# Graph attention over 4096 nodes: another half key group transposed by DMA, adjacency loads issued as a pair, masks made later

## The reference

```python
q = x @ Wq.T + bq; k = x @ Wk.T + bk; v = x @ Wv.T + bv      # x: 4096 x 128, float32
scores = q @ k.T / sqrt(128)
scores = where(adj > 0, scores, -9e15)                       # adj: 4096 x 4096, int32
att = softmax(scores, axis=-1) @ v
return layernorm(x + elu(att), eps=1e-5)                     # no scale or shift
```

## Time and profile before

| | |
|---|---|
| median of 3 runs | 438.9 us (438.66 to 438.95) |
| profiled execution | 439.14 us, of which the span from first to last instruction is 437.3 us |
| busy share of the span | PE 97%, DVE 82%, ACT 82%, POOL 79% |
| DMA | 105.29 MB, mean 241 GB/s; 64 DMA transposes, 64 adjacency loads of 1 MB |
| granted TensorE clock | 0.997 |

### The profile page before, as it was taken

How to read it: one execution, slowest core, us unless ns; L and a number is a source line. 1 busy time by engine, 2 the same in 40 slices (tenths; PEclk the granted TensorE clock), 3 DMA queues, 4 the chain that set the end, 5 groups by cost and what they waited for, 6 DMA issues and landing times.

```text
span 437.3 us, 11386 instructions
## 1 busy us (share of the span) xinstructions
PE 423.0 (97%) x3471; PEld 308.8 (71%) x3471; DVE 359.4 (82%) x665; ACT 357.8 (82%) x739; POOL 346.2 (79%) x617
## 2 busy tenths in 40 slices
PE   8998999999999999999999999999999999999974
PEld 5563676677777777777777777777777777777764
DVE  1759988888889888888889898888889998888723
ACT  5778687888888988888888898888888898888992
POOL 0064567898888988898888988889888888889884
PEclk9999999999999999999999999999999999999998
DMA  8822999999999999999999999999999999997553
GB/s 225 374 98 97 202 252 271 264 262 279 289 274 265 261 244 273 263 269 256 253 276 269 264 245 261 279 259 265 244 271 272 266 252 250 275 265 184 96 103 67
DMA packets 152013, 105.29 MB, mean 241 GB/s; under 512 B 135104, under 2 KB 143808, under 8 KB 143808
## 3 DMA queue, kind: packets, MB, share of 16 engines
q1 hardware_dynamic: 151568, 104.94, 91.0%
q10 hardware_dynamic: 432, 0.20, 0.2%
HBM read 69.47 MB, written 2.10 MB: 164 GB/s over the span
## 4 chain that ended last, share of the span: by engine, by line
PE 82%; DMA 5%; SPq 3%; DVE 3%; ACT 2%; issue 2%; POOL 2%; POOLq 0%; ACTq 0%; DVEq 0%
PE ps_out L721 22%; PE ps_scores L682 11%; PE ps_scores L683 11%; PE ps_scores L684 11%; PE ps_out L723 11%; PE ps_t L698 11%; DMA p_turned<-p_rows 4%; SPq L234 3%; PE ps_t L626 2%; DVE scores L528 2%; PE ps_out L637 1%; DMA x_rows<-in_x_dram 1%; PE ps_out L626 1%; PE ps_scores L648 1%; DVE adj L514 1%
## 5 line engine op out<-in xcount | busy, mean ns | idle before, releaser
L290 POOL TENSOR_TENSOR p_rows<-scores,p_rows 128x256 f16<-128x256 f32 x256 | 178.5, 729 | 13.0 <-ACT p_rows L431 13.0
L528 DVE CUSTOM_DVE_ANT_0 scores<-ps_scores,adj 128x1024 f32<-128x1024 f32 x128 | 155.9, 1218 | 14.2 <-issue 10.8
L414 ACT ACTIVATE scores<-scores,neg_max 128x1024 f32<-128x1024 f32 x128 | 145.6, 1138 | 0.0
L543 DVE TENSOR_TENSOR p_lo<-ps_t,p_hi 128x512 f16<-128x512 f32 x128 | 85.0, 684 | 36.7 <-ACT p_hi L423 36.4
L514 DVE TENSOR_SCALAR adj<-adj 128x1024 f32<-128x1024 int32 x128 | 104.8, 818 | 0.8 <-DMA adj<-in_adj_dram 0.7
L721 PE MATMUL ps_out<-v_parts,p_hi 128*128 128x256 f16 x512 | 98.5, 273 | 1.5 <-DVE p_lo L543 1.1
L721 PE MATMUL ps_out<-v_parts,p_turned 128*128 128x256 f16 x512 | 98.0, 273 | 0.6 <-DMA p_turned<-p_rows 0.4
L682 PE MATMUL ps_scores<-k_hi,q_hi 128*128 128x512 f16 x256 | 97.0, 379 | 1.0 <-DVE max_parts L528 0.9
L683 PE MATMUL ps_scores<-k_lo,q_hi 128*128 128x512 f16 x256 | 97.0, 379 | 0.0
L684 PE MATMUL ps_scores<-k_hi,q_lo 128*128 128x512 f16 x256 | 97.0, 379 | 0.0
L723 PE MATMUL ps_out<-v_parts,p_lo 128*128 128x128 f16 x512 | 91.4, 219 | 0.0
(11 more groups left out here) (70 smaller groups left out, 440.4 us busy)
## 6 DMA issues: line engine op xcount, KB each, us to landing
adj<-in_adj_dram SPq DMA_DIRECT2D x64, 1024.0 KB, 5.3
out_dram<-y_out SPq DMA_DIRECT2D x32, 64.0 KB, 4.9
x_rows<-in_x_dram SPq DMA_DIRECT2D x4, 256.0 KB, 4.3
x_rows<-in_x_dram SPq DMA_DIRECT2D x2, 512.0 KB, 6.3
p_turned<-p_rows SPq DMA_TRANSPOSE x64, 4.5
w_rows<-in_L_gnn_Wk_dram ACTq DMA_DIRECT2D x1, 64.0 KB, 2.7
w_rows<-in_L_gnn_Wq_dram ACTq DMA_DIRECT2D x1, 64.0 KB, 3.3
w_rows<-in_L_gnn_Wv_dram ACTq DMA_DIRECT2D x1, 64.0 KB, 4.0
```

The costliest lines, as they stand in the source:

```text
L290: last = nc.gpsimd.tensor_tensor(p_rows[c][:, w:][:, cols], s_sb[s][:, c * PIECE:c * PIECE + w][:, cols], p_rows[c][:, 0:w][:, cols], ALU. ...
L414: nc.scalar.activation(s_sb[s][:, cols], s_sb[s][:, cols], ACT.Exp, bias=neg_max[:, s:s + 1], accum_out=p_sums[:, s, c:c + 1]).then_inc(ex ...
L528: nc.vector.tensor_tensor_reduce(out=s_sb[s][:, cols], in0=ps_scores[c % 2][:, :], in1=mask_sb[s][:, cols], scale=SCALE, scalar=-3.0e38, o ...
L543: nc.vector.tensor_tensor(p_lo[:, k, :], ps_t[bank_of(s, g)][:, :], p_hi[:, k, :], ALU.subtract).then_inc(plo_ready, 1)
```

## The change

Half of group 4 (256 columns) moves from PE's transposes to the DMA transpose of piece 1, which grows from 1024 to 1280 columns; the half group that is left is transposed by PE in two blocks. POOL's low parts stay operations of 256 columns, so `low_rows(1)` has five. Both loads of an adjacency tile are issued one after the other, behind `turn(p-2, n, 1)`. Each mask is made one step ahead of its use, where it was made half a round ahead. PE's transposes and value products get new steps.

```diff
-DMA_COLS = (PIECE, PIECE)
+MIXED_COLS = 256
+DMA_COLS = (PIECE, PIECE + MIXED_COLS)
...
-T_AT = {4: 6, 5: 7, 6: 8, 7: 10}
-PV_ORDER = (4, 5, 6, 0, 1, 7, 2, 3)
+T_AT = {4: 6, 5: 6, 6: 8, 7: 9}
+PV_STEPS = ((5,), (), (6,), (7, 0), (1,), (2,), (3,), (4,))
+PV_ORDER = tuple(g for step in PV_STEPS for g in step)
...
-LOW_PARTS = 4
+LOW_COLS = 256
...
+        def by_pe(g):
+
+            return slice(MIXED_COLS, BANK) if g == MIXED else slice(0, BANK)
...
                 if turns_1:
                     turn(p - 2, n, 1)
-                if head:
+                if loads:
+                    load_half(p + 1, 1 - n, 0, False)
                     load_half(p + 1, 1 - n, 1, False)
                 if stores:
                     store(p - 4, n)
                 if turns_0:
                     turn(p - 1, 1 - n, 0)
-                if loads:
-                    load_half(p + 2, n, 0, False)
...
-                for b in range(LOW_PARTS):
-                    cols = slice(b * w // LOW_PARTS, (b + 1) * w // LOW_PARTS)
+                for b in range(w // LOW_COLS):
+                    cols = slice(b * LOW_COLS, (b + 1) * LOW_COLS)
...
-                    if c < BY_DMA:
-                        dve.wait_ge(rows_lo, BY_DMA * (i - 2) + c + 1)
+                    if 2 * c <= MIXED:
+                        dve.wait_ge(rows_lo, BY_DMA * (i - 2) + min(c + 1, BY_DMA))
...
-                    if j == 1 and has_scores:
-                        mask_piece(p, n, 3)
-                    if j in (3, 5, 7) and has_scores and makes_mask:
-                        mask_piece(p + 1, 1 - n, j // 2 - 1)
+                    if j in (1, 3, 5) and has_scores:
+                        mask_piece(p, n, j // 2 + 1)
+                    if j == 7 and has_scores and makes_mask:
+                        mask_piece(p + 1, 1 - n, 0)
```

More of the change, by code:

```diff
@@ L20 @@
 LOG_P_SCALE = 15.0 * math.log(2.0)
-DMA_COLS = (PIECE, PIECE)
+MIXED_COLS = 256
+DMA_COLS = (PIECE, PIECE + MIXED_COLS)
 BY_DMA = len(DMA_COLS)
 FIRST_PE = sum(DMA_COLS) // BANK
+MIXED = FIRST_PE
 PE_GROUPS = STEPS - FIRST_PE
-T_AT = {4: 6, 5: 7, 6: 8, 7: 10}
-PV_ORDER = (4, 5, 6, 0, 1, 7, 2, 3)
+T_AT = {4: 6, 5: 6, 6: 8, 7: 9}
+PV_STEPS = ((5,), (), (6,), (7, 0), (1,), (2,), (3,), (4,))
+PV_ORDER = tuple(g for step in PV_STEPS for g in step)
 POOL_OPS = 11
-LOW_PARTS = 4
+LOW_COLS = 256
 LAST_OPS = 9
@@ L234, in turn, with period @@
                 sp.dma_start_transpose(p_turned[c][s][:, :, :], p_rows[c][:, :]).then_inc(turned[c], 16)
-            def period(p, n, head=True, turns_0=True, turns_1=True, stores=True, loads=True):
+            def period(p, n, turns_0=True, turns_1=True, stores=True, loads=True):
                 if turns_1:
                     turn(p - 2, n, 1)
-                if head:
+                if loads:
+                    load_half(p + 1, 1 - n, 0, False)
                     load_half(p + 1, 1 - n, 1, False)
@@ L245, in period @@
                     turn(p - 1, 1 - n, 0)
-                if loads:
-                    load_half(p + 2, n, 0, False)
             load(0, 0)
             load(1, 1)
-            period(0, 0, head=False, turns_0=False, turns_1=False, stores=False)
             period(1, 1, turns_1=False, stores=False)
@@ L257, in _ @@
                     period(2 * pair + n, n)
[L258 to L261, removed]
+            period(TILES - 2, 0)
+            period(TILES - 1, 1, loads=False)
+            period(TILES, 0, loads=False)
+            period(TILES + 1, 1, turns_0=False, loads=False)
             store(TILES - 2, 0)
@@ L422, in high_part @@
                     act.wait_ge(pv_done, pv_count(i - 1, g))
-                nc.scalar.activation(p_hi[:, k, :], ps_t[bank_of(s, g)][:, :], ACT.Copy).then_inc(phi_ready, 1)
+                nc.scalar.activation(p_hi[:, k, by_pe(g)], ps_t[bank_of(s, g)][:, by_pe(g)], ACT.Copy).then_inc(phi_ready, 1)
             def high_rows(i, s, c, first):
                 w = DMA_COLS[c]
-                act.wait_ge(exp_done, exp_count(i, c))
+                act.wait_ge(exp_done, exp_count(i, (c * PIECE + w - 1) // PIECE))
                 if not first:
@@ L542, in low_part @@
                 dve.wait_ge(phi_ready, PE_GROUPS * i + k + 1)
-                nc.vector.tensor_tensor(p_lo[:, k, :], ps_t[bank_of(s, g)][:, :], p_hi[:, k, :],
+                nc.vector.tensor_tensor(p_lo[:, k, by_pe(g)], ps_t[bank_of(s, g)][:, by_pe(g)], p_hi[:, k, by_pe(g)],
                                         ALU.subtract).then_inc(plo_ready, 1)
@@ L598, in period @@
                         reciprocal(p - 2, n)
-                    if j == 1 and has_scores:
-                        mask_piece(p, n, 3)
-                    if j in (3, 5, 7) and has_scores and makes_mask:
-                        mask_piece(p + 1, 1 - n, j // 2 - 1)
+                    if j in (1, 3, 5) and has_scores:
+                        mask_piece(p, n, j // 2 + 1)
+                    if j == 7 and has_scores and makes_mask:
+                        mask_piece(p + 1, 1 - n, 0)
             for n in range(AHEAD):
                 low_of_projection(n)
-                if n > AHEAD - PIECES:
-                    mask_piece(0, 0, n - AHEAD + PIECES - 1)
+                if n == AHEAD - 1:
+                    mask_piece(0, 0, 0)
             period(0, 0, has_1=False, has_2=False, warm=False)
@@ L695, in transposes @@
                     pe.wait_ge(plo_ready, PE_GROUPS * i + k - 1)
-                for b in range(BLOCKS):
+                for b in range(by_pe(g).start // P, BLOCKS):
                     kb = g * BLOCKS + b
@@ L704, in values @@
                     pe.wait_ge(plo_ready, PE_GROUPS * i + g - FIRST_PE + 1)
-                elif g % 2 == 0 or pv_count(0, g - 1) > pv_count(0, g):
-                    pe.wait_ge(turned[g // 2], 16 * i + 16)
+                if g <= MIXED and (g % 2 == 0 or pv_count(0, g - 1) > pv_count(0, g)):
+                    pe.wait_ge(turned[min(g // 2, BY_DMA - 1)], 16 * i + 16)
                 if g == PV_ORDER[0] and not first:
@@ L714, in values @@
                     k = g * BLOCKS + b
-                    if g >= FIRST_PE:
+                    c = min(g // 2, BY_DMA - 1)
+                    if b * P >= by_pe(g).start and g >= FIRST_PE:
                         high = p_hi[:, g - FIRST_PE, b * P:(b + 1) * P]
@@ L718, in values @@
                     else:
-                        high = p_turned[g // 2][s][:, g % 2 * BLOCKS + b, :]
-                        low = p_turned[g // 2][s][:, DMA_COLS[g // 2] // P + g % 2 * BLOCKS + b, :]
+                        high = p_turned[c][s][:, k - c * PIECE // P, :]
+                        low = p_turned[c][s][:, DMA_COLS[c] // P + k - c * PIECE // P, :]
                     nc.tensor.matmul(ps_out[s][:, 0:2 * D], high, v_parts[:, k, :],
@@ L741, in period @@
                             transposes(p - 1, 1 - n, g, not warm)
-                    if has_2:
-                        values(p - 2, n, PV_ORDER[j], first)
+                    for g in PV_STEPS[j]:
+                        if has_2:
+                            values(p - 2, n, g, first)
             period(0, 0, has_1=False, has_2=False, warm=False)
```

## The result

The median went from 438.92 us (438.66 to 438.99) to **515.0 us** (514.5 to 515.28), a ratio of 1.173 [1.172, 1.175]. The forecast was 448.8 us, at most 458: the sign was right, the size wrong by a factor of more than seven (+76 for +10).

The account below looks back on a forecast made before the run. PE bounded the kernel, POOL 3.5% behind; the change would make POOL's 12.61 us loop the pace. 439.14 + 8.9 (rounds) + 2.0 (end) - 1.0 (start) = 449.0 us profiled, 448.8 median; range 438 to 458.

Parts of the forecast that it names:

- The step that failed: On PE: two fewer transposes a tile remove 7.0 us in all, leaving 12.0 us a round, with other work unchanged.
- what costs nothing: DVE's smaller low part, masks, load deadlines, new waits of `masked_piece(2)` and `high_rows(1)`, and the later store: no added time.
- the second loop: From the end of `y` through ACT's copies, DVE's low part and masked piece, exponentials and POOL back to `y`: 12.57 us.
- POOL's loop: POOL's own work and waits in a round: 11.80 us before, 11.80 + 0.63 + 0.18 = 12.61 us after the change.
- the two terms that were forecast: On POOL, each round: 0.63 us for one more 256-column operation, and 0.18 us later start behind ACT's longer copy.
- single-operation bound: Lower bound of POOL's round with the added operation and nothing for ACT's longer copy: 12.43 us.
- POOL at some 95%: Sign expected in the middle stretch: POOL busy some 95% of the time.
- the likeliest case: Rounds set by loops of 12.4 to 12.8 us, 443 to 455 us in all; chance 0.56.
- `res` to the end of `y`: Last term in the sum of the second loop, on POOL: 1.80 us.
- (a): Rival: PE sets the round at 12.0 us, 432 us, or 434 with some waiting; chance 0.12.
- (b): Rival: DVE's masks move off POOL's operations into its waits; rounds of 12.2 us, some 437 to 440 us; chance 0.12.
- (c): Rival: the DMA queue becomes the bound at 12.9 to 13.35 us a round; 458, up to 471 us; chance 0.16.

Follow-up runs that it names:

- e9_copy_ahead_of_row_sum: Changed kernel with two places for group 4, group 7's products one step later, and ACT copying piece 1 ahead of `row_sum`: 446.03 us, ratio 1.015.
- e10_mean_on_act: As e9_copy_ahead_of_row_sum, and ACT's row sum gives the negative mean, so POOL's `neg_mean` is left out: 437.15 us, ratio 0.997.
- e5: Changed kernel with two places for group 4 and group 7's value products at step 4 instead of step 3: 451.95 us, ratio 1.031.
- e7: As e5, with the fifth low part (256 columns) made by DVE at step 7 instead of POOL: 459.49 us, ratio 1.046.

## Why the prediction was wrong

**The step that failed** is "The new steps for transposes and values keep PE's work otherwise as it is", and with it the part on what costs nothing, which followed the waits that the diff writes and no wait that was already there. `high_part` waits for `pv_done` in both kernels. Before, group 4 was multiplied first and copied late in the next round, so that wait never ended last, and no view of the trace had a row for it. The change made the read last. In the sum of the second loop the copy of group 4 stands with 0.25 us and as free to start; in truth it waits 2.27 us. By the experiments this costs 1.72 us a round (14.68 to 12.96). The right sign is no credit to the mechanism: most of the 76 us come from waits that the forecast didn't name, and only the kernel without them is slower for the reason that it gave.

**The second omission** is of the same kind: group 7's products at step 3 close a loop through `masked_piece(0)`. The prediction read the earlier trace rows, where PE's weight loads already wait 0.4 us a round on low parts, and didn't ask what an earlier step does to that wait. Cost: 0.92 to 0.96 us a round on PE; 0.34 (12.96 to 12.62) until POOL takes over.

The miss against the profiled execution (514.5 us) is 65.5 us: 28 x (14.69 - 12.61) = 58.2 in the rounds, 4.2 at the start (+3.2 for -1.0) and 3.2 at the end (+5.2 for +2.0). With both stalls gone the start and the end fall to +0.2 and (449.7 - 414.81) - (437.3 - 405.19) = +2.8, so they too hold mostly the same two waits.

**Right, once the stalls are out of the way:**
- PE's work is 12.04 us, by subtracting the stalls (12.0 was forecast).
- POOL's loop is 12.62 (12.61), made of the two terms that were forecast. The single-operation bound was 12.43, and 12.47 was measured. That the sum is so close is in part luck: the sum kept the masks' collisions as they were, and they moved. `att` takes 0.90 and `res` 0.46, where `res` took 0.90 before, and these two cancel. The sign "POOL at some 95%" didn't come: POOL is busy 43.89 of 50 us, since the waits inside its own loop (0.51 and 0.49 us a round) count as idle.
- Masks and loads cost nothing in the kernel before.
- The kernel without the stalls takes 451.95 us, inside the likeliest case's 443 to 455. The forecast was for a kernel that this change isn't.

**The second loop** exists, but 12.57 us was too much for it: with DVE's 0.82 added it takes 12.88, so some 12.06 without, an estimate from that one difference. It was not measured alone. The term that was too long is "`res` to the end of `y`", put at 1.80: there it takes 247.11 + 0.45 - 246.23 = 1.33 us, because no mask falls on `res`.

**The rivals.** (a), PE as the pace, asked of POOL 0.6 us; only shortening POOL's loop brought it near, and then the mean round is 12.07. (b), masks that move off POOL, happened in part and gained nothing. In the kernel with two places and group 7 later, the mask at 243.81 falls into POOL's wait behind `y`, as (b) had it, and `neg_mean` takes 0.19 where it took 0.57; but the run behind it then waits 0.49 for ACT's copy. Where POOL's order shifts, masks come back. In `e9_copy_ahead_of_row_sum`, POOL's and DVE's timelines show it:

```profile
249.19 0.90 POOL L306 TENSOR_TENSOR att_sum<-att 128x128 f32<-128x128 f32 x1
254.46 0.78 POOL L319 TENSOR_TENSOR y<-res,expm 128x128 f32<-128x128 f32 x1
```

```profile
249.04 0.74 DVE L525 TENSOR_SCALAR adj<-adj 128x1024 f32<-128x1024 int32 x1
254.24 0.69 DVE L525 TENSOR_SCALAR adj<-adj 128x1024 f32<-128x1024 int32 x1
```

Both POOL operations take 0.46 alone, and start while a mask runs that has 0.59 and 0.47 us to go; they take 0.44 and 0.32 longer. The Trainium skill (SBUF — State Buffer, Who interferes with whom) has the later instruction stand still for the whole of the other, if VectorE's is in a two-port mode; these rows agree in kind and are 0.15 us short of it each. (c), the DMA queue, was not the bound: the DMA share fell to 0.84. Without the stalls it is back at 0.99, and where POOL's loop is shorter too, ACT's copies wait for landings (a row of the waits each, before, then `e9_copy_ahead_of_row_sum` and `e10_mean_on_act`):

```profile
ACT p_rows L431 <- DMA p_turned<-p_rows: 4.6, 4, 2.1
```

```profile
ACT p_rows L442 <- DMA p_turned<-p_rows: 11.9, 24, 1.8
```

```profile
ACT p_rows L440 <- DMA p_turned<-p_rows: 9.9, 15, 3.0
```

So the queue is close behind PE and POOL there. That one change between kinds of transfer fewer saves anything, as the prediction held against (c), no run shows.

## What to carry to other kernels

When a step is moved, list every wait of the instructions that read or write its buffers, above all the write-after-read waits that never end last and so have no row in the trace; for a buffer with one place per round, a reader moved from first to last in the round holds up the next writer, and everything queued behind that writer. Then ask of each moved consumer which of its own engine's later results its producer needs first. A second place, or a reader two steps earlier, is cheap: here either gave back over 52 us. And where the bound engine has 3.5% of lead, moving 2% of its work onto the next engine only makes that one the bound.

## What the runs showed that was not expected

- Order alone, with no instruction added, costs 14% (438.9 to 501.9 us): three short ACT instructions (250.03 to 252.16 in the changed kernel) stop PE in every round.
- The gain on PE, 28 x (12.23 - 12.04) = 5.3 us, came here only with four further edits, and 2.4 us of it are measured. In the profiled execution one late landing takes 14.36 - 12.07 = 2.3 us, and the end 33.6 (435.1 - 401.54) for 32.1 us. It is no chance of one execution: in the four kernels in which group 4 has two places and group 7 stands later (the runs e5, e7, e9 and e10) the fourth round is the longest, with 13.03, 13.19, 13.54 and 14.36 us, and in each ACT's copy waits for a landing then, 0.50, 0.21, 1.83 and 3.03 us. What makes the transpose land late there wasn't tried.
